# Score bias, mean times rstd and the soul shift as per-partition-scalar operations on VectorE

## Chip, cores and metric

The kernel runs on one core of one Trainium2 chip. The metric is the device time of one execution in microseconds (us), lower is better. Engines are called PE (TensorE matmul; PEld its weight loads), DVE (VectorE), ACT (ScalarE), POOL (GpSimd) and SP (the DMA-issuing SyncE).

## What is computed

128 graphs of 128 nodes with 256 features go through four layers, each with its own weights:

```
L0: softmax(q k^T / sqrt(32) + log(clip(adj, 1e-8))) v  in 8 heads, then @ Wo.T + bo, then layer_norm(x + out)
L1: p = x @ fc_w.T + fc_b ; q = p.q_w + q_b ; k = p.k_w + k_b
    masked = q + k^T + (1 - adj) * -1e9 ; leaky relu 0.01 ; softmax @ p + x
L2: scores = Q K^T / sqrt(32) + a[:, :, None] + c[:, None, :] + b_g + log(adj + 1e-9)
    with a = x @ w_g[:256], c = x @ w_g[256:] ;  softmax @ V + x
L3: as L1, with weights of its own
```

Three small steps of this matter here. The *score bias* is the sum of q_b and k_b with the node scores of L1 and L3. *Mean times rstd* is the layer norm's offset: x is normed as `x * rstd + less`, with `less = -mean * rstd`. The *soul shift* is the per-node term a (`soul` in the kernel) that is carried through the row extreme of the L2 scores.

## The kernel before

The 128 graphs are worked in 64 groups of two (`GROUP = 2`). A group passes through some 35 named steps on PE, 38 on DVE, 39 on ACT, 10 on POOL and 2 on SP. Several groups are in flight: a table `ORDER` gives, for each engine, the steps of one period with a lag, so that in the period of group t DVE does, for instance, `norm` of group t and `qk 3` of group t-3. Tables `EARLY` and `LATE` give the order at both ends. Each engine runs its list in order, and every dependence between engines is a semaphore wait written by hand ahead of the step. All matmul outputs go to eight PSUM banks of fixed use.

The steps that are touched:

- `qk` ("1" and "3" for L1 and L3), DVE, line 1092: once ACT has copied both graphs' projections to `fp` (line 839), it adds `qk_b` to the two score columns `fp[..., 256:258]`, q and k, in place, and raises `qk_ready`. PE's step `mask` (line 1313) then turns the k column of each graph into a row by two transposes, and DVE's `mask` (line 959) adds row, q column and penalty.
- `max_parts B`, DVE, lines 1006 and 1010: from the row extremes `least_B` of the L2 scores (four `max B` steps, line 1000) it makes `top = soul - least`, then `least_cols = soul - top`, with a wait of DVE on its own first instruction between the two. PE's step `turn_max B` (line 1279) transposes `least_cols_B`; ACT copies it (`least_rows_B`, line 775) and PE's `shift B` (line 1199) uses it.
- `norm`, DVE, line 1077: after POOL's power (`rstd`, line 700) one instruction makes `less` for both graphs and raises `centred`; ACT's `norm` (line 771, one instruction for each graph) writes `x_1`, and PE's `turn_x 1` (line 1285) transposes it.
- SP's loading order at the start: the first group's inputs, then eight weight tensors, then the rest.

PE also runs idle matmuls (`keep_awake`, line 1263) at both ends of the program. They write only scratch values.

Of the kernel before, what the change touches and what calls it, by code (L numbers as in the profile page):

```python
# [6 lines left out]
ALU = mybir.AluOpType  # L7
# [3 lines left out]
P = 128  # L11
GROUP = 2
# [309 lines left out]
def build_kernel(nc, ins, out):  # L322
# [4 lines left out]
    with ExitStack() as ctx:  # L327
# [36 lines left out]
        least = {"B": sb("least_B", [P, HALF, UNITS])}  # L364
        top = sb("top", [P, HALF, UNITS])
        least_cols = {s: sb(f"least_cols_{s}", [P, HALF, HEAD_DIM]) for s in "AB"}
# [77 lines left out]
        maxed = {s: sem(f"maxed_{s}") for s in "AB"}  # L444
        topped = sem("topped")
        least_ready = {"B": sem("least_ready_B")}
# [122 lines left out]
        def _(sp):  # L569
# [19 lines left out]
            load_weight("k0")  # L589
            first, *others = steps("sync")  # L590
            step(first[0], first[3])
            for n in ("o0", "f1", "k2", "q2", "f1_rows", "f3_rows", "v2", "f3"):
                load_weight(n)
            for name, _, _, G in others:
                step(name, G)
            for i in range(2):
                sp.wait_ge(stored[i], 16 * len(range(i, GROUPS, 2)))
# [112 lines left out]
        def _(act):  # L710
# [37 lines left out]
            def program():  # L748
                for name, where, n, G in steps("scalar"):
# [18 lines left out]
                    elif name == "norm":  # L768
                        act.wait_ge(centred, G.no + 1)
                        for g in range(GROUP):  # L770
# [51 lines left out]
                    elif name == "v":  # L822
                        act.wait_ge(filled[b], fills.after(G, *key))
                        if where == "0":
                            act.activation(v["A"][:, G.odd, :, :].rearrange("p g d -> p (g d)"), bank[b][:, :],
                                           ACT.Copy).then_inc(v_ready["A"], 1)
                        else:
                            act.activation(v["B"][:, G.odd, n, :], bank[b][:, 0:WIDE], ACT.Copy
                                           ).then_inc(v_ready["B"], 1)
                            if n == GROUP - 1:  # L830
                                act.wait_ge(v_ready["B"], GROUP * (G.no + 1))
                                G.wait_former(act, least_ready["B"], 1, 2)
                                act.activation(soul[:, G.odd, :], v["B"][:, G.odd, :, DIM], ACT.Identity,
                                               bias=soul_b[:, 0:1]).then_inc(soul_ready, 1)
                                act.activation(c_cols[:, :, 0:GROUP], v["B"][:, G.odd, :, DIM + 1].unsqueeze(1).broadcast_to(
                                    [P, HALF, GROUP]), ACT.Copy).then_inc(c_cols_ready, 1)
# [35 lines left out]
        def _(dve):  # L872
# [79 lines left out]
            def mask(layer, G):  # L952

                key = ("mask", layer, 0)
                b = BANK[key]
                dve.wait_ge(penalty_ready, G.no + 1)
                dve.wait_ge(filled[b], fills.after(G, *key))
# [31 lines left out]
            def program():  # L989
                for name, where, n, G in steps("vector"):  # L990
# [11 lines left out]
                    elif name == "max_parts" and where == "B":  # L1002
                        dve.wait_ge(maxed[where], HALF * (G.no + 1))
                        dve.wait_ge(soul_ready, G.no + 1)
                        a = soul[:, G.odd, :].unsqueeze(2).unsqueeze(1).broadcast_to([P, HALF, GROUP, 2])
                        dve.tensor_tensor(top[:, :, :].rearrange("p r (g h) -> p r g h", g=GROUP), a,
                                          least["B"][:, :, :].rearrange("p r (g h) -> p r g h", g=GROUP),
                                          ALU.subtract).then_inc(topped, 1)
                        dve.wait_ge(topped, G.no + 1)
                        dve.tensor_tensor(least_cols["B"][:, :, 0:UNITS].rearrange("p r (g h) -> p r g h", g=GROUP),  # L1010
                                          a, top[:, :, :].rearrange("p r (g h) -> p r g h", g=GROUP),
                                          ALU.subtract).then_inc(least_ready["B"], 1)
                    elif name == "adj_t":
# [61 lines left out]
                    elif name == "norm":  # L1075
                        dve.wait_ge(rstd_ready, G.no + 1)
                        dve.scalar_tensor_tensor(less[:, :], moments[:, :, 0], -1.0, rstd[:, :], ALU.mult, ALU.mult
                                                 ).then_inc(centred, 1)
                    elif name == "turn_x" and where != "0":
# [8 lines left out]
                    elif name == "qk":  # L1088

                        dve.wait_ge(fp_ready[where], GROUP * (G.no + 1))  # L1090
                        qk = fp[where][:, :, DIM:WIDE]
                        dve.tensor_tensor(qk, qk, qk_b[where][:, :].unsqueeze(1).broadcast_to([P, GROUP, 2]), ALU.add
                                          ).then_inc(qk_ready[where], 1)
# [13 lines left out]
        def _(pe):  # L1107
# [157 lines left out]
            def other(name, layer, n, G, to):  # L1265
# [8 lines left out]
                if name == "turn_max":  # L1274
                    if layer == "A":
                        pe.wait_ge(maxed["A"], HALF * (G.no + 1))
                    else:
                        pe.wait_ge(least_ready["B"], G.no + 1)
                    return pe.transpose(to[:, 0:P], least_cols[layer][:, :, :].rearrange("p r c -> p (r c)"),  # L1279
# [29 lines left out]
                if name == "mask":  # L1309

                    pe.wait_ge(qk_ready[layer], G.no + 1)
                    for g in range(GROUP):
# [93 lines left out]
```

## Time and profile before

| what | value |
|---|---|
| median of the runs of before | 1796.31 us (3 runs, 1795.67 to 1799.39) |
| profiled execution, first to last instruction | 1798.2 us |
| median less the profiled span | -1.9 us |
| PE busy | 1757.7 us, 98% |
| DVE busy | 1475.6 us, 82% |
| ACT busy | 1372.0 us, 76% |
| POOL busy | 731.3 us, 41% |

The profile records one execution. Busy time is a share of its span; the span is the profiled execution's own time, and no other time is recorded of it. The three runs are others, without the profiler. A row of a timeline has the start, the duration, the engine, the line and the operation with its tiles, and in brackets how long the engine sat idle before it and what ended that.

### The profile page before, as it was taken

To read this page: it belongs to the slowest core of one execution; us is meant where nothing else is said; L and a number is where in the kernel's file an instruction comes from. 1 tells how busy PE (TensorE), PEld (TensorE's weight loads), DVE (VectorE), ACT (ScalarE), POOL (GpSimd) and SP (SyncE) were. 2 spreads that over 40 slices of the span, in tenths; PEclk is the share of its full clock that TensorE was granted. 3 is DMA by queue.
4 is the path that set the end of the run, shared out by engine and by line. 5 is a ranking of instruction groups with operands and counts; after the bars stand their busy time and mean duration, and the time that the engine had idled before them with its cause. 6 is when DMAs were issued, how large, how long until landed. Compare 5 with 4: busy or idle time off the path is not lost.

```text
span 1798.2 us, 68824 instructions
## 1 busy us (share of the span) xinstructions
PE 1757.7 (98%) x28155; PEld 1647.2 (92%) x28155; DVE 1475.6 (82%) x3361; ACT 1372.0 (76%) x3792; POOL 731.3 (41%) x797
## 2 busy tenths in 40 slices
PE   7999999999999999999999999999999999999997
PEld 6899999999999999999999999999999999999986
DVE  4688888888888888888888888888888888888875
ACT  3677787777787787787787787787787787787774
POOL 3343344343443343443443343343443443443421
PEclk8999999999999999999999999999999999999999
DMA  3101011011011011011011011011011011011100
GB/s 116 39 20 49 26 49 49 26 49 50 26 49 49 26 49 49 27 49 49 26 49 50 26 49 50 26 49 49 26 49 49 26 49 49 26 49 49 35 8 25
DMA packets 48261, 74.56 MB, mean 41 GB/s; under 512 B 5456, under 2 KB 21968, under 8 KB 47952
## 3 DMA queue, kind: packets, MB, share of 16 engines
q1 hardware_dynamic: 47376, 69.49, 12.1%
q8 instruction: 228, 3.74, 0.9%
q14 instruction: 81, 0.66, 0.1%
q10 hardware_dynamic: 576, 0.68, 0.1%
HBM read 53.37 MB, written 16.78 MB: 39 GB/s over the span
## 4 chain that ended last, share of the span: by engine, by line
PE 87%; ACT 3%; DMA 3%; DVE 3%; issue 2%; POOL 2%; SPq 0%; DVEq 0%; POOLq 0%; ACTq 0%
PE banks L1111 15%; PE banks L1176 14%; PE banks L1113 13%; PE banks L1112 13%; PE banks L1325 7%; PE banks L1220 6%; PE banks L1211 6%; DMA x_t<-x_t_dram 3%; PE banks L1199 2%; PE banks L1285 2%; PE banks L1225 2%; PE banks L1313 1%; PE banks L1319 1%; POOL weights_B L684 1%; PE banks L1279 1%
## 5 line engine op out<-in xcount | busy, mean ns | idle before, releaser
L684 POOL TENSOR_TENSOR weights_B<-weights_B,adj 128x512 f32<-128x512 f32 x64 | 113.0, 1766 | 299.1 <-ACT weights_B L765 299.1
L690 POOL TENSOR_TENSOR inv_parts_A<-inv_both_A,own 128x512 fp32r<-128x512 f32 x64 | 66.7, 1042 | 303.7 <-DVE inv_both_A L1035 303.7
L1000 DVE TENSOR_REDUCE least_cols_A<-banks 128x4 f32<-128x512 f32 x256 | 159.4, 684 | 33.8 <-PE banks L1176 33.7
L1000 DVE TENSOR_REDUCE least_B<-banks 128x4 f32<-128x512 f32 x256 | 172.6, 681 | 11.6 <-PE banks L1185 11.5
L1111 PE MATMUL banks<-w_hi_v,xt_hi 128*128 128x258 f32 (+1 forms) x512 | 157.3, 307 | 9.5 <-DVE pick L883 9.5
L1111 PE MATMUL banks<-w_hi_f,xt_hi 128*128 128x258 f32 x512 | 162.3, 317 | 2.3 <-DVE xt_lo L875 0.7
L839 ACT ACTIVATE fp<-banks 128x258 f32<-128x258 f32 x256 | 92.6, 390 | 89.1 <-PE banks L1113 89.1
L765 ACT ACTIVATE banks<-banks,v_B 128x256 f32<-128x256 f32 x384 | 153.4, 474 | 0.0
L1111 PE MATMUL banks<-xt_hi,w_hi_k 128*128 128x256 f32 x512 | 150.7, 294 | 0.3 <-DVE xt_lo L875 0.3
L1113 PE MATMUL banks<-w_lo_v,xt_hi 128*128 128x258 f32 (+1 forms) x512 | 145.1, 283 | 0.0
L1112 PE MATMUL banks<-w_hi_v,xt_lo 128*128 128x258 f32 (+1 forms) x512 | 145.0, 283 | 0.0
L1113 PE MATMUL banks<-w_lo_f,xt_hi 128*128 128x258 f32 x512 | 144.9, 283 | 0.0
L1112 PE MATMUL banks<-xt_hi,w_lo_k 128*128 128x256 f32 x512 | 144.2, 282 | 0.0
L1112 PE MATMUL banks<-w_hi_f,xt_lo 128*128 128x258 f32 x512 | 143.8, 281 | 0.0
L1113 PE MATMUL banks<-xt_lo,w_hi_q 128*128 128x256 f32 x512 | 143.8, 281 | 0.0
L1111 PE MATMUL banks<-xt_hi,w_hi_q 128*128 128x256 f32 x512 | 143.7, 281 | 0.0
L1113 PE MATMUL banks<-xt_lo,w_hi_k 128*128 128x256 f32 x512 | 143.6, 280 | 0.0
L1112 PE MATMUL banks<-xt_hi,w_lo_q 128*128 128x256 f32 x512 | 143.6, 280 | 0.0
L1325 PE MATMUL banks<-fpt,fp 128*128 128x128 f32 x1024 | 142.1, 281 | 1.2 <-ACT fpt L860 1.0
L1325 PEld LDWEIGHTS banks<-fpt,fp 128*128 128x128 f32 x1024 | 128.3, 191 | 14.8 <-issue 12.4
L1024 DVE TENSOR_TENSOR weights_A<-banks,adj 128x512 f32<-128x512 f32 x192 | 125.7, 683 | 9.2 <-ACT banks L761 9.2
L1031 DVE RECIPROCAL banks<-banks 128x128 f32<-128x128 f32 x128 | 122.4, 956 | 9.3 <-PE banks L1220 9.3
(192 smaller groups left out, 6172.0 us busy)
## 6 DMA issues: line engine op xcount, KB each, us to landing
x_t<-x_t_dram SPq DMA_DIRECT2D x64, 256.0 KB, 3.6
x_in<-x_dram SPq DMA_DIRECT2D x64, 256.0 KB, 3.6
out_dram<-x_out SPq DMA_DIRECT2D x64, 256.0 KB, 2.4
adj_t<-adj_t_dram SPq DMA_DIRECT2D x64, 128.0 KB, 3.4
adj<-adj_dram SPq DMA_DIRECT2D x64, 128.0 KB, 2.0
scratch<-weights_dram SPq DMA_DIRECT2D x9, 256.0 KB, 6.6
scratch<-weights_dram ACTq DMA_DIRECT2D x2, 256.0 KB, 4.3
out_bias<-L_gnn_bo_dram ACTq DMA_DIRECT2D x1, 128.0 KB, 7.8
```

Source lines behind the costliest of these rows:

```text
L684: pool.tensor_tensor(units, units, weight_of[where][:, G.four, :, :].unsqueeze(2).broadcast_to([P, GROUP, 2, P]), ALU.mult).then_inc(first ...
L765: last = act.activation(to[:, cols(g, 2 * P)], x[:, cols(g, 2 * P)], ACT.Exp, bias=v["B"][:, G.odd, g, DIM + 1:WIDE], scale=-1.0)
L1000: dve.tensor_reduce(to, bank[SCORE_BANKS[n]].rearrange("p (u m) -> p u m", u=UNITS), axis=AX.X, op=ALU.min).then_inc(maxed[where], 1)
L1024: dve.tensor_tensor(weights[where][:, n, :].rearrange(units, g=GROUP, h=2), bank[SCORE_BANKS[n]].rearrange(units, g=GROUP, h=2), weight_of ...
L1031: dve.reciprocal(bank[b][:, 0:P], bank[b][:, 0:P]).then_inc(inverted[where], 1)
L1111: pe.matmul(out_ap, left_hi(k), right_hi(k), start=(k == 0), stop=False)
L1112: pe.matmul(out_ap, left_lo(k), right_hi(k), start=False, stop=False)
L1113: last = pe.matmul(out_ap, left_hi(k), right_lo(k), start=False, stop=(k == KT - 1))
L1176: last = pe.matmul(bank[SCORE_BANKS[r]][:, cols(u)], left[row_group(r), G.odd, half, cols(g)], right[row_group(r), G.odd, half, cols(g)], ...
L1211: last = pe.matmul(to[row_group(r), cols(u)], v[s][:, G.odd, g, head:head + HEAD_DIM], weights[s][:, r, cols(u)], start=True, stop=True)
L1220: last = pe.matmul(to[row_group(r), 0:P], sums[:, u, :], weights[s][:, r, cols(u)], start=(u == 0), stop=(u == UNITS - 1), skip_group_chec ...
L1325: last = pe.matmul(to[:, cols(k * GROUP + g)], fp[layer][:, g, cols(k)], fpt[layer][:, g, :], start=True, stop=True)
```

## The change

`qk` becomes one `tensor_scalar` for each layer that adds both biases (two per-partition scalars) to the q column alone; PE's `mask` step no longer waits for it, but only for ACT's `fp`, and DVE's `mask` step waits for it by name. `max_parts B` becomes two `tensor_scalar`, one for each graph, that subtract and add `soul` and don't depend on each other; tile `top` and its semaphore are gone. `norm` becomes two `tensor_scalar`, one for each graph. All steps keep their places. SP's start is written as another loop with the same order.

```diff
-        top = sb("top", [P, HALF, UNITS])
...
-                        act.wait_ge(centred, G.no + 1)
+                        act.wait_ge(centred, GROUP * (G.no + 1))
...
-                                G.wait_former(act, least_ready["B"], 1, 2)
+                                G.wait_former(act, least_ready["B"], GROUP, 2)
...
                 b = BANK[key]
+                dve.wait_ge(qk_ready[layer], G.no + 1)
                 dve.wait_ge(penalty_ready, G.no + 1)
...
-                        a = soul[:, G.odd, :].unsqueeze(2).unsqueeze(1).broadcast_to([P, HALF, GROUP, 2])
-                        dve.tensor_tensor(top[:, :, :].rearrange("p r (g h) -> p r g h", g=GROUP), a,
-                                          least["B"][:, :, :].rearrange("p r (g h) -> p r g h", g=GROUP),
-                                          ALU.subtract).then_inc(topped, 1)
-                        dve.wait_ge(topped, G.no + 1)
-                        dve.tensor_tensor(least_cols["B"][:, :, 0:UNITS].rearrange("p r (g h) -> p r g h", g=GROUP),
-                                          a, top[:, :, :].rearrange("p r (g h) -> p r g h", g=GROUP),
-                                          ALU.subtract).then_inc(least_ready["B"], 1)
+                        for g in range(GROUP):
+                            dve.tensor_scalar(least_cols["B"][:, :, 2 * g:2 * g + 2], least["B"][:, :, 2 * g:2 * g + 2],
+                                              soul[:, G.odd, g:g + 1], soul[:, G.odd, g:g + 1],
+                                              ALU.subtract, ALU.add).then_inc(least_ready["B"], 1)
...
-                        dve.scalar_tensor_tensor(less[:, :], moments[:, :, 0], -1.0, rstd[:, :], ALU.mult, ALU.mult
-                                                 ).then_inc(centred, 1)
+                        for g in range(GROUP):
+                            dve.tensor_scalar(less[:, g:g + 1], moments[:, g, 0:1], rstd[:, g:g + 1], -1.0,
+                                              ALU.mult, ALU.mult).then_inc(centred, 1)
...
-                        qk = fp[where][:, :, DIM:WIDE]
-                        dve.tensor_tensor(qk, qk, qk_b[where][:, :].unsqueeze(1).broadcast_to([P, GROUP, 2]), ALU.add
+                        q = fp[where][:, :, DIM]
+                        dve.tensor_scalar(q, q, qk_b[where][:, 0:1], qk_b[where][:, 1:2], ALU.add, ALU.add
                                           ).then_inc(qk_ready[where], 1)
...
-                        pe.wait_ge(least_ready["B"], G.no + 1)
+                        pe.wait_ge(least_ready["B"], GROUP * (G.no + 1))
...
-                    pe.wait_ge(qk_ready[layer], G.no + 1)
+                    pe.wait_ge(fp_ready[layer], GROUP * (G.no + 1))
```

DVE in a middle period, from the last `max B` to the L3 `mask`, before the change (in brackets the semaphores that the instruction waits for):

```order
L1000 TENSOR_REDUCE least_B<-banks 128x4 [waits filled0]
L1092 TENSOR_TENSOR fp<-fp,cols_tile 128x2x2 [waits fp_ready_3]
L1006 TENSOR_TENSOR top<-soul,least_B 128x16 [waits soul_ready,maxed_B]
L1010 TENSOR_TENSOR least_cols_B<-soul,top 128x4x4 [waits topped]
L1041 TENSOR_TENSOR banks<-banks,heads_A 128x512 [waits filled5,heads_ready_A]
L986 TENSOR_TENSOR sum_t<-banks,xb_t 128x512 [waits filled6,x3_ready,x_biased_1]
L959 SCALAR_TENSOR_TENSOR logits<-banks,fp,penalty 128x128 [waits filled7,penalty_ready]
```

The same stretch of DVE after the change:

```order
L998 TENSOR_REDUCE least_B<-banks 128x4 [waits filled0]
L1087 TENSOR_SCALAR fp<-fp,cols_tile 128x2 [waits fp_ready_3]
L1004 TENSOR_SCALAR least_cols_B<-least_B,soul 128x4x2 [waits soul_ready,maxed_B]
L1004 TENSOR_SCALAR least_cols_B<-least_B,soul 128x4x2
L1035 TENSOR_TENSOR banks<-banks,heads_A 128x512 [waits filled5,heads_ready_A]
L984 TENSOR_TENSOR sum_t<-banks,xb_t 128x512 [waits filled6,x3_ready,x_biased_1]
L957 SCALAR_TENSOR_TENSOR logits<-banks,fp,penalty 128x128 [waits filled7,penalty_ready,qk_ready_3]
```

The count of instructions is the same here; the wait for `topped` is gone, and the first `mask` instruction has `qk_ready_3` as a third wait.

DVE around `norm` in the same period, before the change:

```order
L1072 TENSOR_SCALAR rstd<-moments 128x1 [waits stats_ready,moments_ready,x1_ready]
L1074 BN_AGGR moments<-stats 128x2
L1087 RECIPROCAL f_inv<-f_den 128x2 [waits f_exped_3]
L1077 SCALAR_TENSOR_TENSOR less<-moments,rstd 128x2 [waits rstd_ready]
L1000 TENSOR_REDUCE least_cols_A<-banks 128x4 [waits filled0] x4
```

And after it:

```order
L1066 TENSOR_SCALAR rstd<-moments 128x1 [waits stats_ready,moments_ready,x1_ready]
L1068 BN_AGGR moments<-stats 128x2
L1082 RECIPROCAL f_inv<-f_den 128x2 [waits f_exped_3]
L1072 TENSOR_SCALAR less<-moments,rstd 128x1 [waits rstd_ready]
L1072 TENSOR_SCALAR less<-moments,rstd 128x1
L998 TENSOR_REDUCE least_cols_A<-banks 128x4 [waits filled0] x4
```

There is one instruction more ahead of the four `max A`.

PE around the L3 `mask` and `turn_max B`, before the change:

```order
L1325 MATMUL banks<-fpt,fp 128x128 x3
L1313 MATMUL banks<-ident,fp 128x128 [waits qk_ready_3,fpt_ready_1]
L1313 MATMUL banks<-ident,fp 128x128
L1279 MATMUL banks<-ident,least_cols_B 128x128 [waits least_ready_B,fp_ready_3]
L1176 MATMUL banks<-qt_B,kt_B 128x128 [waits maxed_B]
```

And after it:

```order
L1320 MATMUL banks<-fpt,fp 128x128 x3
L1308 MATMUL banks<-ident,fp 128x128 [waits fp_ready_3,fpt_ready_1]
L1308 MATMUL banks<-ident,fp 128x128
L1274 MATMUL banks<-ident,least_cols_B 128x128 [waits least_ready_B,fp_ready_3]
L1171 MATMUL banks<-qt_B,kt_B 128x128 [waits maxed_B]
```

Nothing moves on PE; one wait names ACT's semaphore instead of DVE's.

## Rows read from the trace of the kernel before

**Rows 1.** The page: busy time, share of the span and instructions of each engine.

```profile
PE 1757.7 (98%) x28155; PEld 1647.2 (92%) x28155; DVE 1475.6 (82%) x3361; ACT 1372.0 (76%) x3792; POOL 731.3 (41%) x797
```

**Rows 2.** Windows: stretch, length, busy by engine, PE clock share, DMA share, GB/s.

```profile
0.00:60.00 60.00, 44.21 (x484) 40.33 (x485) 29.26 (x70) 24.50 (x55) 21.21 (x47) 0.86 0.31 102
800.00:1200.00 400.00, 398.93 (x6502) 375.46 (x6495) 340.10 (x774) 316.74 (x880) 170.05 (x178) 1.00 0.13 40
1200.00:1600.00 400.00, 396.45 (x6489) 372.81 (x6491) 335.88 (x769) 313.04 (x869) 167.65 (x177) 1.00 0.13 42
1740.00:1798.20 58.20, 47.39 (x627) 41.44 (x625) 33.40 (x73) 31.30 (x91) 10.83 (x12) 1.00 0.05 20
```

**Rows 3.** PE's waits, whole span: waited for, us in total, times, longest.

```profile
PE banks L1285 <- ACT x L771: 9.0, 12, 1.6
...
PE banks L1279 <- DVE least_cols_B L1010: 0.2, 1, 0.2
PE banks L1313 <- DVE fp L1092: 0.2, 1, 0.2
```

**Rows 4.** PE's waits in the window 400 to 1600 us, all of them.

```profile
PE banks L1285 <- ACT x L771: 5.9, 8, 1.6
PE banks L1225 <- POOL inv_parts_B L690: 0.2, 1, 0.2
```

**Rows 5.** Timeline around `qk 3` and `max_parts B` of a middle period.

```profile
923.60 0.16 DVE L1092 TENSOR_TENSOR fp<-fp,cols_tile 128x4 f32<-128x4 f32 x1 [0.30 <-ACT fp L839]
923.67 0.17 DVE L1006 TENSOR_TENSOR top<-soul,least_B 128x16 f32<-128x16 f32 x1
923.88 0.17 DVE L1010 TENSOR_TENSOR least_cols_B<-soul,top 128x16 f32<-128x16 f32 x1
923.98 0.69 DVE L1041 TENSOR_TENSOR banks<-banks,heads_A 128x512 f32<-128x512 f32 x1
...
924.10 0.38 PE L1313 MATMUL banks<-ident,fp 128*128 128x128 f32 x2
...
924.31 0.27 PE L1279 MATMUL banks<-ident,least_cols_B 128*128 128x128 f32 x1
```

**Rows 6.** Timeline around `norm` in a period where PE waited.

```profile
717.77 0.16 DVE L1077 SCALAR_TENSOR_TENSOR less<-moments,rstd 128x2 f32<-128x2 f32 x1 [1.10 <-POOL rstd L700]
...
718.45 2.48 DVE L1000 TENSOR_REDUCE least_cols_A<-banks 128x4 f32<-128x512 f32 x4 [0.52 <-PE banks L1176]
...
720.16 0.63 ACT L794 ACTIVATE xt_hi<-x_t 128x512 fp32r<-128x512 f32 x1 [1.15 <-DMA x_t<-x_t_dram]
...
720.70 1.07 ACT L771 ACTIVATE x<-x,less,rstd 128x256 f32<-128x256 f32 x2
...
721.91 0.63 PE L1285 MATMUL banks<-ident,x 128*128 128x128 f32 x4 [0.73 <-ACT x L771]
```

**Rows 7.** Chain that ended last, at the last group's `qk 3`: start, us, what.

```profile
1787.66 0.40 ACT fp L839
1788.06 0.02 issue
1788.08 0.18 DVE fp L1092
1788.26 0.04 issue
1788.30 0.45 PE banks L1313 x2
```

**Rows 8.** The same chain at the first group's `max_parts B`.

```profile
85.47 0.47 DVE top L1006
...
85.96 0.18 DVE least_cols_B L1010
```

**Rows 9.** Waits: who waited for `less`, in total, times, longest.

```profile
ACT x L771 <- DVE less L1077: 1.9, 3, 1.0
```

**Rows 10.** DVE groups by form: busy us, mean ns, then idle time before.

```profile
L1035 DVE SCALAR_TENSOR_TENSOR inv_both_B<-banks,low_row,inv_hi_B 128x128 f32<-128x128 f32 x64 | 22.5, 351 | 2.2
...
L1072 DVE TENSOR_SCALAR rstd<-moments 128x1 f32<-128x1 f32 x64 | 9.8, 154 | 5.8
```

More of the change, by code:

```diff
@@ L444, in build_kernel @@
         maxed = {s: sem(f"maxed_{s}") for s in "AB"}
-        topped = sem("topped")
         least_ready = {"B": sem("least_ready_B")}
@@ L589, in _ @@
             load_weight("k0")
[L590 to L594, printed above, removed]
+            for i, (name, _, _, G) in enumerate(steps("sync")):
                 step(name, G)
+                if i == 0:
+                    for n in ("o0", "f1", "k2", "q2", "f1_rows", "f3_rows", "v2", "f3"):
+                        load_weight(n)
             for i in range(2):
```

## The prediction

> **What bounds the kernel now.** I read the page's first part first: PE is busy for 1757.7 of 1798.2 us, DVE for 82% [rows 1]. A high busy share alone can mislead, since it is a mean over stages, so the second view is the table of windows. In the middle of the program PE is busy for 398.9 and 396.5 us of two stretches of 400 us; at the two ends it is busy for 44.2 of 60.0 and 47.4 of 58.2 us [rows 2]. The reader is to see two different regimes: a middle in which a DVE edit can win only what PE waits there, and two ends in which single instructions lie one behind another.
>
> The third view is the list of what PE waited for. In the 1200 us from 400 to 1600 it has two entries: ACT's `x` (step `norm`), 5.9 us in 8 waits, and a POOL tile, 0.2 us in one wait [rows 4]. None names DVE. Over the whole span the two DVE products that the change touches and PE reads, `least_cols_B` and `fp`, held PE up once each, for 0.2 us [rows 3]. So 128 `mask` steps and 64 `turn_max B` steps on PE have practically no wait to give back.
>
> The one large wait does touch an edited step: `turn_x 1` on PE for ACT's `x`, 9.0 us in 12 waits [rows 3]. The timeline of such a period tells why it happens. `less` was written at 717.93 (717.77 plus 0.16), but ACT began `x` only at 720.70, because ACT first stood 1.15 us for the DMA of `x_t`, which its preceding instruction needs [rows 6]. The transfer is late, not `less`. ACT waited for `less` only 3 times in 64 groups, 1.9 us in all [rows 9].
>
> **The change, part by part.**
>
> *Score bias.* One DVE instruction stands for one, of 0.16 us before [rows 5]; the new one handles 2 elements instead of 4, and the nearest tensor_scalar, on one element, takes 154 ns [rows 10]. DVE's time is unchanged. What changes is that PE's `mask` starts after ACT's `fp`. In the middle `qk 3` ends at 923.76 and PE takes up the transposes at 924.10 [rows 5], behind its own matmuls: 0.34 us of cover, nothing gained. In the last group the pair is on the chain: ACT's `fp` ends at 1788.06, DVE's bias takes 1788.08 to 1788.26, PE begins at 1788.30 [rows 7]. Without the bias in between PE begins at about 1788.10, if its hand-over from ACT takes the 0.04 us that it takes from DVE: a gain of 0.20 us, once. The bias is then done beside the transposes (0.45 us [rows 7]), and DVE's `mask`, which now waits for it by name, finds it done. Behind this wait on DVE stand `mask`, `weigh` and `leak`; as DVE works in order, the bias, issued ahead of them, has been finished for long in the middle too.
>
> *Soul shift.* Two instructions stand for two. Before, the second began 0.21 us after the first (923.67 to 923.88), while the next instruction, which doesn't depend on it, followed after 0.10 (923.88 to 923.98), and the first had itself followed `qk` after 0.07 (923.60 to 923.67) [rows 5]. The self-wait thus costs some 0.11 us. After: the second ends at about 923.67 + 0.09 + 0.16 = 923.92 instead of 924.05, 0.13 us sooner. PE wants the tile at 924.31 [rows 5], so nothing is gained in the middle, and DVE's own 0.1 us in each group goes into its idle share. In the first group the pair is on the chain, 0.47 and 0.18 us [rows 8]; I take 0.15 us of gain there. The bounds are none, if the 0.47 us is a cost of the first execution of that place in the program, and 0.4, if it goes away with the chain.
>
> The Trainium skill ("VectorE: DVE Perf Modes", section "The DRAIN you can't avoid") holds that a semaphore after each of a row of DVE instructions costs nothing over one at the end. By it the 0.15 us would be zero and the sum 0.15 us higher. This trace doesn't agree for these tiny dependent instructions: 0.21 against 0.10 us from start to start [rows 5].
>
> *Mean times rstd.* One instruction becomes two. Its price in DVE's stream is one more start-to-start distance, 0.07 to 0.10 us as above [rows 5]; I take 0.09, and 0.18 as an upper end, when the second shows the whole instruction. In the middle DVE sits idle for 0.52 us right behind `less`, until PE's scores are there [rows 6], so the four `max A` begin at the same time as before. ACT has room as well: without its 1.15 us for the DMA it would have begun `x` at 719.55 instead of 720.70, still 1.6 us after `less` was there [rows 6]. On the path it lies in the places where ACT did wait, three of them [rows 9]: 3 times 0.09 is 0.27 us of loss, at most 0.54.
>
> *SP's loop, the tile and the semaphore that go* change no order. I put them at nothing.
>
> **The sum.** -0.20 (bias, last group) -0.15 (soul shift, first group) +0.27 (mean times rstd, three places) is -0.08 us against a profiled execution of 1798.2 us. Its span lies 1.9 us above the median of the three runs, which is more than the whole effect, so I carry the difference to the median: 1796.31 - 0.08 is **1796.2 us**. The bounds of the terms, taken all to one side, are -0.20 - 0.4 + 0 = -0.6 and 0 + 0 + 0.54 = +0.5 us.
>
> **Rivals.**
>
> *Slower, because a new pair ends after PE wants it.* This has one place, `turn_max B`. No row shows a DVE instruction with two per-partition scalars. The nearest with one is `inv_both`, 351 ns, though on 128 elements [rows 10]; the longest in this place is 0.47 us [rows 8]. The point that decides is 924.31, where PE takes up the tile: the pair now ends 0.26 us ahead of it [rows 5]. With 0.47 us and a second start to start of 0.47 the second ends at 924.61, 0.30 us too late, in each of 64 groups: 19 us, 1815 us. Against it: 128 elements alone account for much of the 351 ns, and eight elements are little; the one-element tensor_scalar takes 154 ns [rows 10]. 0.03.
>
> *Slower, by the number of instructions.* 64 more DVE instructions at 0.09 us are 5.8 us, 1802.1 us, if DVE's stream set the pace. It decides where less than 0.09 us of idle time follows `less`; the row shows 0.52 [rows 6], and PE's list has no DVE entry [rows 4]. 0.02. The Trainium skill (same page, section "Rules for kernel authors") advises to minimise the count of operations rather than of semaphores, which speaks for this rival; the rows of this kernel say that DVE has room for them.
>
> *Faster, by the whole wait for `x`.* If the 12 waits were owed to `less`, or if DVE's 0.1 us per group brought the `x_t` transfer forward, up to 9.0 us [rows 3] would come back: 1787.3 us. Against it: the releaser is the DMA [rows 6], and that is issued by SP in an order and behind waits that the change leaves alone. 0.03.
>
> *Nothing at all at the ends.* The chain has other branches within tenths of a microsecond, so that the -0.20 and -0.15 may be swallowed and the +0.27 too: 1796.3 us. This can't be told apart from my forecast by a timing; it shares its chance.
>
> **How the numbers follow.** The three runs of before lie 3.7 us apart, 0.2%; a change below about 0.2%, 3.6 us, can't be told from no change. My forecast, with the case of nothing at the ends, has 0.92, and falls within 0.2% unless the runs themselves stray. The rivals have 0.03, 0.02 and 0.03. I move 0.01 more to each side for edges at which DVE's slightly shifted stream meets a bank or a transfer in a way that the rows don't show: faster 0.04, same 0.90, slower 0.06. The range holds the forecast, the -0.6 and +0.5 of the terms and a spread like that of the runs: 1796.31 - 0.6 - 1.5 is 1794.2, and 1799.39, the slowest run of before, less a little, 1798.9. The rivals with 0.08 lie outside.
>
> **What the next profile would show.** Right: PE's waits between 400 and 1600 us again with no DVE entry and some 6 us for `x`; DVE's instructions up by 64; starts of the soul pair 0.07 to 0.10 us apart; `less` twice and still idle time behind it; on the last chain ACT's `fp` handing over to PE directly. Wrong: a wait of PE for `least_cols_B` in many groups with per-partition-scalar instructions of 0.3 us or more (first rival); the idle time ahead of `max A` gone (second); the `x` waits gone (third).

## The result, and the profile after

The changed kernel takes 1815.26 us (median of 4 runs, 1813.92 to 1815.87) against 1797.37 us for the kernel before on the same chip (4 runs, 1795.67 to 1799.39): a ratio of 1.0098, 95% interval 1.0084 to 1.0112. It is 1% slower. The forecast was 1796.2 us, no change.

The page of the changed kernel, its head and first part (busy time, share of the span, instructions):

```profile
span 1813.3 us, 68888 instructions
...
PE 1772.2 (98%) x28155; PEld 1652.8 (91%) x28155; DVE 1509.9 (83%) x3425; ACT 1372.6 (76%) x3792; POOL 730.6 (40%) x797
```

The profiled execution took 15.1 us more than the one before [rows 1]. PE's share is still 98%, since its busy time has grown by 14.5 us as well. PE did no more work: there are 28155 matmuls in both, and between 400 and 1600 us their mean length is 0.28 us in both. But these records overlap. A matmul is drawn that long while the next usually starts 0.12 us behind it, so PE can be held for a tenth or two without a gap between two records. The share says nothing of the loss. The list of what PE waited for from 400 to 1600 us (engine, tile and line, what ended the wait; us in total, times, longest) says hardly more:

```profile
PE banks L1280 <- ACT x L768: 4.6, 6, 1.2
PE banks L1106 <- DVE xt_lo L872: 0.4, 1, 0.4
PE banks L1274 <- DVE least_cols_B L1004: 0.2, 1, 0.2
```

Beside [rows 4] the DVE tile of the soul shift has appeared, but with one wait of 0.2 us, and 15 us are missing. The same list for the weight loads of the changed kernel has a trace of it, under a name that accuses nobody:

```profile
PEld banks L1171 <- issue: 17.2, 81, 0.3
...
PEld banks L1274 <- issue: 3.9, 23, 0.4
```

The kernel before has no row for `turn_max B` (L1279) in this list. Its row for the scores is longer, not shorter, so that row is no part of the loss:

```profile
PEld banks L1176 <- issue: 20.9, 123, 0.3
```

The view that does show it is the timeline around DVE's `qk 3` and `max_parts B`, the place of [rows 5], in the changed kernel:

```profile
955.07 0.29 DVE L1087 TENSOR_SCALAR fp<-fp,cols_tile 128x2 f32<-128x2 f32 x1 [0.32 <-ACT fp L836]
955.27 0.48 DVE L1004 TENSOR_SCALAR least_cols_B<-least_B,soul 128x8 f32<-128x8 f32 x2
955.46 0.25 PEld L1308 LDWEIGHTS banks<-ident,fp 128*128 128x128 f32 x2
...
955.65 0.69 DVE L1035 TENSOR_TENSOR banks<-banks,heads_A 128x512 f32<-128x512 f32 x1
955.86 0.14 PEld L1274 LDWEIGHTS banks<-ident,least_cols_B 128*128 128x128 f32 x1
```

and the two weight loads of the same place in the kernel before, which [rows 5] leave out:

```profile
923.99 0.25 PEld L1313 LDWEIGHTS banks<-ident,fp 128*128 128x128 f32 x2
...
924.21 0.14 PEld L1279 LDWEIGHTS banks<-ident,least_cols_B 128*128 128x128 f32 x1
```

From the start of the bias to the end of the soul pair it is 0.68 us now (955.07 to 955.75); before it was 0.45 (923.60 to 924.05 [rows 5]). The weight load of `turn_max B` follows the pair after 0.11 us now and followed after 0.16 before. So DVE is 0.23 us longer, the first 0.05 us of that were free here, and the rest is PE's: from the first weight load of `mask` to that of `turn_max B` it is 0.40 us where it was 0.22.

The groups of instructions with their shapes, of the changed kernel (count | busy us, mean ns of one | idle before):

```profile
L1087 DVE TENSOR_SCALAR fp<-fp,cols_tile 128x2 f32<-128x2 f32 x128 | 36.4, 284 | 20.8 <-ACT fp L836 20.8
L1004 DVE TENSOR_SCALAR least_cols_B<-least_B,soul 128x8 f32<-128x8 f32 x128 | 31.1, 288 | 0.3
L1029 DVE SCALAR_TENSOR_TENSOR inv_both_B<-banks,low_row,inv_hi_B 128x128 f32<-128x128 f32 x64 | 22.5, 351 | 2.2
L1072 DVE TENSOR_SCALAR less<-moments,rstd 128x1 f32<-128x1 f32 x128 | 21.4, 209 | 64.4 <-POOL rstd L697 64.4
L1066 DVE TENSOR_SCALAR rstd<-moments 128x1 f32<-128x1 f32 x64 | 9.8, 154 | 6.2 <-DVE moments L1061 0.4
```

The bias instruction, priced by a neighbour of 154 ns, takes 284. The second place that it hurts is `qk 1`, which DVE does ahead of the first row of `weigh A` and `mask 1`. In the changed kernel:

```profile
945.83 0.28 DVE L1087 TENSOR_SCALAR fp<-fp,cols_tile 128x2 f32<-128x2 f32 x1
946.02 1.28 DVE L1018 TENSOR_TENSOR weights_A<-banks,adj 128x512 f32<-128x512 f32 x2
...
947.74 0.68 DVE L1018 TENSOR_TENSOR weights_A<-banks,adj 128x512 f32<-128x512 f32 x1
...
948.01 0.25 PEld L1314 LDWEIGHTS banks<-ident,logits 128*128 128x128 f32 x2
...
948.53 0.90 PEld L1171 LDWEIGHTS banks<-kt_B,qt_B 32*128 32x128 f32 x28 [0.27 <-issue]
```

And in the kernel before:

```profile
914.49 0.15 DVE L1092 TENSOR_TENSOR fp<-fp,cols_tile 128x4 f32<-128x4 f32 x1
914.55 1.28 DVE L1024 TENSOR_TENSOR weights_A<-banks,adj 128x512 f32<-128x512 f32 x2
...
916.27 0.68 DVE L1024 TENSOR_TENSOR weights_A<-banks,adj 128x512 f32<-128x512 f32 x1
...
916.69 0.24 PEld L1319 LDWEIGHTS banks<-ident,logits 128*128 128x128 f32 x2
...
917.10 0.98 PEld L1176 LDWEIGHTS banks<-kt_B,qt_B 32*128 32x128 f32 x32 [0.17 <-issue]
```

The scores of half B overwrite the bank that the last `weigh A` reads. They begin 0.11 us after its end now (948.42 to 948.53) and began 0.15 after it (916.95 to 917.10). The bracket reads "issue" in both kernels, 0.27 us for 0.17. The prediction never looked at this place.

Because the waits hide under weight loads, the rest of this text measures PE by distances: from the first weight load of a step to the first of the next, mean over the 43 whole periods between 400 and 1600 us of each profile, in us. `turn_p` to scores B is the second place (the step is `turn_p 3`, which stands ahead of scores B in PE's order; the expectations below call it `turn_p 1`), `mask 3` to `turn_max B` the first, "col to den" is from the column terms of scores B to `den A`, "x" from the projection ahead of `turn_x 1` to it, where PE waits for ACT's `x`. e1 to e11 are the experiments below.

```
        period  turn_p to  col to   mask 3 to    turn_max B   x
                scores B   den      turn_max B   to again B
before  26.993  0.420      0.457    0.228        0.306        0.907
after   27.242  0.496      0.481    0.408        0.259        0.864
e1      27.105  0.503      0.480    0.301        0.260        0.857
e2      26.988  0.420      0.455    0.301        0.260        0.863
e3      26.903  0.417      0.456    0.232        0.306        0.801
e4      27.040  0.435      0.482    0.340        0.259        0.797
e5      26.941  0.412      0.457    0.222        0.307        0.854
e6      27.133  0.413      0.450    0.220        0.310        0.834
e7      27.111  0.502      0.480    0.220        0.309        0.847
e8      26.934  0.419      0.449    0.221        0.308        0.849
e9      27.087  0.514      0.482    0.225        0.307        0.873
e10     27.067  0.418      0.454    0.296        0.259        0.894
e11     27.009  0.449      0.481    0.221        0.309        0.814
```

The column x scatters by 0.1 us from profile to profile whatever the kernel. The changed kernel's period is 0.249 us longer: +0.180 and -0.047 around `turn_max B`, +0.076 and +0.024 around scores B, -0.043 in x, and +0.059 in many steps of 0.02 us and less. Because x scatters, kernels are better compared by the period less x: +0.292 us for the changed kernel, which times 62 periods is 18 us, about the measured difference. Over the whole program, the 55 periods from the start of the fifth group's scores A (121.7 us in the profile before) to that of the sixtieth (1607.4) are 12.5 us longer, what lies behind them 3.2 longer, the start 0.6 shorter; together 15.1. The 3.2 us are mostly middle periods too: at the last scores B (1766.6 us before) the changed kernel is 14.1 us late, so only about 1 us falls behind that.

### The profile page after: what moved, and what is told of

Same layout as the page of the kernel before. It is cut to its first block, busy times and chain, and to the rows that moved or that the text cites. A ratio compares the mean times of both kernels' runs of the same rounds, so it can differ in the third digit from the quotient of the medians.

```text
span 1813.3 us, 68888 instructions
## 1 busy us (share of the span) xinstructions
PE 1772.2 (98%) x28155; PEld 1652.8 (91%) x28155; DVE 1509.9 (83%) x3425; ACT 1372.6 (76%) x3792; POOL 730.6 (40%) x797
## 4 chain that ended last, share of the span: by engine, by line
PE 87%; DVE 4%; DMA 2%; ACT 2%; issue 2%; POOL 2%; SPq 0%; DVEq 0%; POOLq 0%; ACTq 0%
PE banks L1106 16%; PE banks L1171 14%; PE banks L1108 13%; PE banks L1107 13%; PE banks L1320 7%; PE banks L1215 6%; PE banks L1206 6%; PE banks L1194 2%; DMA x_t<-x_t_dram 2%; PE banks L1220 2%; PE banks L1280 2%; PE banks L1314 2%; PE banks L1308 1%; PE banks L1274 1%; PE banks L1180 1%
```

## The experiments

The theory after the result: an instruction with per-partition scalars costs DVE more than the plain form, and at two places PE waits for DVE's stream with next to no slack. Its rivals: the cost is the changed waits (PE's `mask` for `fp`, DVE's `mask` by name); or it is the number of instructions; or the longer x path. Each ratio is to the kernel before as timed beside it on the same chip, with the 95% interval.

**e1, the bias part alone**, in the kernel before:

```diff
+                dve.wait_ge(qk_ready[layer], G.no + 1)
...
-                        qk = fp[where][:, :, DIM:WIDE]
-                        dve.tensor_tensor(qk, qk, qk_b[where][:, :].unsqueeze(1).broadcast_to([P, GROUP, 2]), ALU.add
+                        q = fp[where][:, :, DIM]
+                        dve.tensor_scalar(q, q, qk_b[where][:, 0:1], qk_b[where][:, 1:2], ALU.add, ALU.add
...
-                    pe.wait_ge(qk_ready[layer], G.no + 1)
+                    pe.wait_ge(fp_ready[layer], GROUP * (G.no + 1))
```

> The kernel before with the score bias alone as changed (bias instruction with two per-partition scalars, PE's mask step waiting for fp only). Theory H (hand-over): PE takes up scores B and turn_max B no sooner than 0.11 to 0.12 us after the DVE instruction that it waits for; before, both stood at 0.15, so 0.04 us was all the slack. The new bias instruction holds DVE 0.19 instead of 0.07 us from start to start, once ahead of the weigh A that scores B waits for and once ahead of the soul pair: 0.08 us each per group, some 0.05 of the second given back behind turn_max B. 0.11 us x 62 groups is 7 us: 1804 us, ratio 1.0035 to 1.005. Rival N (the extra norm instruction is the cause): no change, 1797. Rival P (PE's own changed wait is the cause, whatever DVE's instruction costs): the whole 17 us here, 1815.

1806.61 us, ratio 1.0057 (1.0040 to 1.0074), just above the range that was expected. **e2, the soul part alone** (the hunks of the change for `max_parts B`, `top` left in place):

> The kernel before with the soul shift alone as changed. Theory H: the pair ends 0.10 us later than before (0.55 instead of 0.45 us after the start of the bias instruction ahead of it), of which 0.04 is slack and about 0.05 is given back behind turn_max B: 0 to 1.5 us in all, 1797 to 1799. Rival S (the soul pair alone is the cause, as the first rival of the prediction had it): 12 to 19 us, 1810 to 1816. Rival N: no change.

1799.66 us, 1.0017 (1.0006 to 1.0029). **e3, the norm part alone**:

> The kernel before with mean times rstd alone as changed. Theory H: hidden by the idle time behind it, 0.30 us of which is left in the changed kernel: within 1 us of before, 1797. Rival N (64 more DVE instructions set the pace): 6 to 17 us, 1803 to 1814.

1794.51 us, 0.9995 (0.9984 to 1.0005). The parts add up to 0.69% where the whole costs 0.98%. The table says where the rest is. At `turn_max B` each of e1 and e2 is +0.073 and is given back 0.045 right behind it, a net of 0.03; both together are +0.180 and give back the same 0.047, a net of 0.13. What is given back comes once, whatever the size, so the two parts cost 0.08 us more together than apart, 62 times 0.08 is 5 us or 0.28%. (The intervals of the three parts leave the sum of 0.69% open by about 0.2%; the distances are sharper.)

**e4, one scalar instead of two**: in the changed kernel the sum of the two biases is formed once, in the setup.

```diff
+                    dve.tensor_tensor(q_b[n][:, :], qk_b[n][:, 0:1], qk_b[n][:, 1:2], ALU.add).then_inc(setup_dve, 1)
...
-                        dve.tensor_scalar(q, q, qk_b[where][:, 0:1], qk_b[where][:, 1:2], ALU.add, ALU.add
+                        dve.tensor_scalar(q, q, q_b[where][:, 0:1], None, ALU.add
```

> The changed kernel with one edit: the two biases are summed once at the start, so the bias instruction has one per-partition scalar instead of two. Theory H with a price by the number of per-partition scalars: DVE's duration of the bias falls from 284 to about 206 ns and its start to start from 0.19 to 0.12 us; 0.07 us less at each of two places per group, 4 to 9 us of the 17 come back: 1806 to 1811. If the price lay in the instruction's kind and not in its scalars: 1815, duration 284.

**e5, no scalar**: the kernel before with the new waits of e1 and that summed column, as a tensor_tensor.

```diff
+                        q = fp[where][:, :, DIM]
+                        dve.tensor_tensor(q, q, q_b[where][:, :].broadcast_to([P, GROUP]), ALU.add
```

> The kernel before with PE's mask step waiting for fp only and the bias on the q column alone, as in the change, but as a tensor_tensor with a column that holds the sum of both biases (summed once at the start), so without a per-partition scalar. Theory H (the price lies in the per-partition scalars, and PE meets it at two hand-overs): DVE's bias takes 156 ns again, PE's distance from turn_p 1 to scores B is 0.42 us again (0.50 with the changed bias), and the time is that of before within 0.15%: 1793 to 1798. Rival P (what costs is that PE waits for ACT's fp instead of DVE): 1806, as with the bias change alone.

e4 is 1806.83 us, 1.0057 (1.0041 to 1.0073); e5 is 1798.08 us, 1.0008 (0.9999 to 1.0017). The groups of the bias in e4, and then in e5:

```profile
L1090 DVE TENSOR_SCALAR fp<-fp,q_b 128x2 f32<-128x2 f32 x128 | 28.7, 224 | 21.0 <-ACT fp L837 21.0
```

```profile
L1096 DVE TENSOR_TENSOR fp<-fp,q_b 128x2 f32<-128x2 f32 x128 | 20.2, 158 | 19.6 <-ACT fp L840 19.6
```

On the same two elements: 158, 224 and 284 ns with no, one and two per-partition scalars. From its start to that of DVE's next instruction it is 0.07, 0.13 and 0.19 us. One scalar less in the changed kernel gives back 0.41% (1.0098 to 1.0057); 0.06 us at 128 places is 7.7 us, 0.43%. With e5 the new waits are acquitted: its distances are those of the kernel before. So is the other rival, as far as it is one of counts: in its periods e4 has as many instructions as the changed kernel.

**e6, the last `weigh A` ahead of `mask 1`** in DVE's order of the kernel before. This asks whether scores B is held by DVE for more than the change added.

```diff
-        (3, "sum", "2", 0), (1, "qk", "1", 0), (0, "weigh", "A", 1), (0, "weigh", "A", 2), (1, "mask", "1", 0),
-        (0, "weigh", "A", 3), (1, "leak", "1", 0), ...
+        (3, "sum", "2", 0), (1, "qk", "1", 0), (0, "weigh", "A", 1), (0, "weigh", "A", 2), (0, "weigh", "A", 3),
+        (1, "mask", "1", 0), (1, "leak", "1", 0), ...
```

> The kernel before with one exchange in DVE's order: the third weigh A of a group ahead of mask 1 in the middle periods. Theory H says that PE's scores B is held by this weigh in the kernel before too: its distance from turn_p 1 falls from 0.42 to 0.22 to 0.30 us, 0.12 to 0.2 us per group, 7 to 12 us in all: 1784 to 1789, if what DVE does next has room for mask 1 being 0.6 us later (0.2 us of idle time ahead of max B and 0.3 us ahead of the L3 bias speak for that). Rival: scores B was not held by DVE (the trace names no releaser there): no change at scores B, 1795. Third possibility: scores B starts sooner but the delay of leak 1 reappears at wide A or turn_max B, and the time stays or grows.

1806.97 us, 1.0054 (1.0041 to 1.0066). The gain of 7 to 12 us that was expected is not there: with `weigh A` done a whole instruction sooner, scores B still begins 0.413 us after `turn_p` (0.420 before). In the kernel before DVE holds PE by hundredths at this place at most. The loss is elsewhere: DVE's `mask 1` comes later, DVE then stands 0.52 us ahead of `leak 1`, in the period shown, until ACT has answered it. What follows in DVE's order is late, POOL's `inv_parts_A` with it, and `wide A` on PE begins 0.213 us later in each period (mean distance ahead of it 0.916 for 0.703). The rows of DVE and POOL, of e6:

```profile
945.51 0.42 DVE L968 TENSOR_TENSOR logits<-banks,logits 128x256 f32<-128x256 f32 x1 [0.52 <-ACT banks L842]
...
949.92 1.04 POOL L690 TENSOR_TENSOR inv_parts_A<-inv_both_A,own 128x512 fp32r<-128x512 f32 x1 [4.95 <-DVE inv_both_A L1035]
951.09 0.19 PEld L1225 LDWEIGHTS banks<-inv_parts_A,spread 128*128 128x128 f32 x1
```

**e7, `max_parts B` ahead of `qk 3`** in DVE's order of the changed kernel:

```diff
-        (3, "qk", "3", 0), (2, "max_parts", "B", 0), ...
+        (2, "max_parts", "B", 0), (3, "qk", "3", 0), ...
```

> The changed kernel with one exchange in DVE's order: the L3 bias behind the soul pair instead of ahead of it (PE's mask no longer waits for the bias). Theory H: the pair ends 0.19 us sooner, PE's distance from the L3 mask to turn_max B falls from 0.41 to about 0.23 us, of which 0.05 was given back behind it: 0.13 us per group, 8 us less than the changed kernel, 1805 to 1808, ratio to before 1.0045 to 1.007. If this hand-over were not on PE's path: 1815.

1805.65 us, 1.0046 (1.0034 to 1.0059). `mask 3` to `turn_max B` falls from 0.408 to 0.220, the level of before, with the two-scalar pair as slow as ever: some 0.5% of the 0.98% came from this place.

**e8, the bias on POOL**: the kernel before with the waits of e5 and the bias of both layers in POOL's order.

```diff
+                        pool.tensor_tensor(q, q, q_b[where][:, :].broadcast_to([P, GROUP]), ALU.add
+                                           ).then_inc(qk_ready[where], 1)
```

> As the tensor_tensor bias, but done by POOL (in gaps of its order where it waits for DVE or ACT), so that DVE has no bias at all. Theory H: DVE reaches the weigh A that scores B waits for 0.07 us sooner than before, and the soul pair too: turn_p 1 to scores B 0.42 to 0.35 us, the L3 mask to turn_max B 0.23 to 0.21: 0.07 to 0.09 us per group, 4 to 6 us less than before: 1790 to 1792. Rival: POOL delivers the bias too late for DVE's mask and the time grows by some microseconds.

1795.43 us, 0.9990 (0.9981 to 0.9999). The expected gain of 4 to 6 us did not come. With no bias on DVE at all the two distances are what they were, and the gain is 0.1%: from the level of before the way down is flat.

**e9 and e10, two spare instructions without scalars** ahead of DVE's `qk 1` (e9) and of `qk 3` (e10) in the kernel before. They write a tile that nobody reads:

```diff
+                            for i in range(2):
+                                dve.tensor_tensor(spare[:, i, :], one[:, :].broadcast_to([P, 2]),
+                                                  big[:, :].broadcast_to([P, 2]), ALU.add)
```

> The kernel before with two more DVE instructions (tensor_tensor on 2 elements of tiles that nothing else uses, no per-partition scalar) ahead of the L1 bias of every group. They hold DVE for 2 x 0.07 = 0.14 us, a little more than the 0.12 us by which the changed bias is longer. Theory H: scores B goes 0.10 us later (turn_p 1 to scores B 0.42 to 0.52), 6 us in all, 1803, ratio 1.003 to 1.004. Rival: DVE's room absorbs it, since the kernel before has 4 us of DVE idle time per group: 1796.

> As the run before it, but the two instructions stand ahead of the L3 bias. Theory H: turn_max B goes 0.10 us later (L3 mask to turn_max B 0.23 to 0.33), of which 0.05 is given back behind it: 3 us, 1798 to 1800, ratio 1.001 to 1.003. Rival: absorbed, 1796.

e9 is 1805.77 us, 1.0051 (1.0039 to 1.0063); e10 is 1803.11 us, 1.0041 (1.0029 to 1.0053). Plain instructions that hold DVE for 0.14 to 0.15 us lengthen the same distances by about as much as the scalars' 0.12 us: +0.094 and +0.025 around scores B (e1 +0.083 and +0.023), +0.068 ahead of `turn_max B` (e1 +0.073). It is DVE's lateness that counts, whatever it is made of. In time both came out above the ranges expected, and together they cost 0.92% where e1 costs 0.57%. For e10 a part of that can be read from its trace: in the kernel before, PE's `mask 3` still waits for DVE's bias. In e10 it begins 0.116 us after the bias ends in the mean, 0.115 at least (0.224 or more before), which is the least distance that a hand-over takes here, and the step ahead of it is 0.029 us longer. So e10 holds a third hand-over, which the changed kernel doesn't have.

**e11, e4 and e7 together**:

> The changed kernel with both remedies: the biases summed once, so that the bias instruction has one per-partition scalar, and the L3 bias behind the soul pair. Theory H: scores B 0.43 us after turn_p 1 and turn_max B 0.22 us after the L3 mask, as before; the time is that of before within 0.2%: 1795 to 1800. If something else in the change cost time (the norm instruction, the sum of small shifts elsewhere), some microseconds stay.

1801.48 us, 1.0023 (1.0013 to 1.0034), a little more than expected. `turn_max B` is at the level of before; scores B, which was expected at 0.43 us, keeps +0.029 and +0.024, since the one scalar is still there. The rest is 0.01 us here and there, in projections, `mix` and the output projection.

**e12, `x_t` earlier**: from the third group on, SP issues a group's `x_t` ahead of its `adj` in the kernel before, not behind it. This tests how the prediction read PE's one large wait.

```diff
-                    G.wait_former(sp, xt_ready["0"], 1, 1)
-                    sp.dma_start(x_t[:, :], ins["x_t"][G.no]).then_inc(xt_landed, 16)
+                    if G.no < 2:
+                        G.wait_former(sp, xt_ready["0"], 1, 1)
+                        sp.dma_start(x_t[:, :], ins["x_t"][G.no]).then_inc(xt_landed, 16)
...
+                    if 0 < G.no < GROUPS - 1:
+                        sp.wait_ge(xt_ready["0"], G.no + 1)
+                        sp.dma_start(x_t[:, :], ins["x_t"][G.no + 1]).then_inc(xt_landed, 16)
```

> The kernel before with one transfer moved in SP's order: from the third group on x_t of the next group is issued ahead of the adj transfer that waits for POOL's penalty step, so some 20 us sooner. It tests the prediction's reading that PE's waits for ACT's x (9.0 us in 12 waits) are owed to late x_t transfers. If so, these waits nearly vanish from the trace, PE's distance from den B to turn_x falls from 0.91 us to 0.8 or below in the mean, and the time falls by 4 to 8 us: 1789 to 1793, ratio 0.9955 to 0.998. If they are owed to something else (ACT's own queue): 1796.

1792.42 us, 0.9975 (0.9966 to 0.9984), faster than both kernels. PE's wait for `x` and, from the groups by line, ACT's for the transfer, of e12:

```profile
PE banks L1289 <- ACT x L775: 1.7, 3, 1.0
```

```profile
L798 ACT ACTIVATE xt_hi<-x_t 128x512 fp32r<-128x512 f32 x64 | 40.3, 630 | 0.8 <-DMA x_t<-x_t_dram 0.8
```

The same group of ACT in the kernel before:

```profile
L794 ACT ACTIVATE xt_hi<-x_t 128x512 fp32r<-128x512 f32 x64 | 40.4, 631 | 12.9 <-DMA x_t<-x_t_dram 12.9
```

9.0 us in 12 waits [rows 3] have become 1.7 in 3, and ACT's wait for the transfer has gone from 12.9 to 0.8 us. The distance x is 0.72 us in the mean (0.91 before), the other distances are those of before. DVE's part in `norm` is untouched.

## Why the prediction was wrong

**The step that failed is the price of the bias**: "the new one handles 2 elements instead of 4, and the nearest tensor_scalar, on one element, takes 154 ns [rows 10]. DVE's time is unchanged." That neighbour has immediates for operands. The bias takes 284 ns and holds up the next instruction by 0.19 us for 0.07. The trace of the kernel before had the price, in two pairs of instructions of the setup that differ only in this: line 913 takes a per-partition scalar (`minus_gamma`) for one layer and an immediate for the other.

```profile
L913 DVE SCALAR_TENSOR_TENSOR w_lo_f<-banks,minus_gamma,w_hi_f 128x2 fp32r<-128x2 f32 x2 | 0.3, 214 | 1.9 <-ACT w_hi_f L732 1.9
L913 DVE SCALAR_TENSOR_TENSOR w_lo_f<-banks,w_hi_f 128x2 fp32r<-128x2 f32 x2 | 0.2, 149 | 0.0
```

That is 65 ns for one scalar on two elements. Two of them on the 159 ns of the old bias give an estimate of 289; 284 and 288 were measured. `inv_both`, with one per-partition scalar, 351 ns on 128 elements [rows 10], says the same. DVE's big forms here give the cost of an element: 683 ns on 512 and 422 on 256 is 1.02 ns each; 128 of them are 131 ns, which leaves 220 for the scalar form. e4 measured 224. The prediction waved it off with "128 elements alone account for much of the 351 ns" and didn't do this subtraction. The soul shift fell with it: each of its pair takes 288 ns, so from its own start the pair takes 0.48 us for the 0.38 of the old form, and ends 0.10 later, not 0.13 sooner. The self-wait that it saves is less than the scalars cost (e2).

**The cover was read at the wrong row.** The "0.26 us ahead" and "0.34 us of cover" run up to the start of the matmuls (924.31, 924.10 [rows 5]). What waits first is the weight load, 924.21, and a load never followed its DVE instruction by less than 0.11 us. The slack was 924.21 less 0.11 less 924.05, 0.05 us here; over 45 periods the mean distance was 0.147 us where the floor is 0.115 (0.114 to 0.116 in all 44 periods of the changed kernel), so 0.03. About the same slack stood at scores B (0.150 for 0.115), which the prediction didn't visit at all. "None names DVE" was true of the list of waits and told little, since a hold of a tenth of a microsecond is put down to "issue" or covered by overlapping records.

**The first rival was right in its kind.** It named the place (`turn_max B`), the form (two per-partition scalars), and the sign that would show it, "instructions of 0.3 us or more" (0.28 and 0.29), and gave 1815 us for the 1815.26 measured, at a chance of 0.03. The closeness of the number is luck: its 19 us were 0.30 us at one place; what happened is 0.13 net there, 0.10 at scores B and 0.06 in small steps, in each period. Its price should have been 65 ns for each scalar, and its point of decision 0.05 us, not 0.26; both could be read from the trace of the kernel before, and with them a loss was to be forecast. Its second sign, "a wait of PE for `least_cols_B` in many groups", did not appear between 400 and 1600 us (one wait named, 23 as "issue").

**The second rival**, by the number of instructions, is not what happened: e3 adds the same 64 instructions and costs nothing. The place decides: 128 instructions more ahead of `qk 1` (e9) cost 0.51%. The Trainium skill ("VectorE: DVE Perf Modes", section "Rules for kernel authors") advises to minimise the count of operations. Taken alone that would have pointed at `norm`, the one part with more instructions, and these runs don't bear it out there; e4 has the count of the changed kernel in its periods and is 0.4% faster.

**Mean times rstd** was right: room behind `less`, no change (0.9995). In the changed kernel, ACT's waits for `less`, then the timeline behind it:

```profile
ACT x L768 <- DVE less L1072: 2.2, 3, 1.2
```

```profile
937.73 0.33 DVE L1072 TENSOR_SCALAR less<-moments,rstd 128x1 f32<-128x1 f32 x2 [1.10 <-POOL rstd L697]
938.37 2.48 DVE L998 TENSOR_REDUCE least_cols_A<-banks 128x4 f32<-128x512 f32 x4 [0.30 <-PE banks L1171]
```

Three waits again, 2.2 us for 1.9 [rows 9], +0.3 as the +0.27 of the sum (three waits are few, and e3's time can't tell a term of this size from none), and 0.30 us of idle time left for 0.52 [rows 6]. The instruction is 209 ns where one on the same single element with immediates alone is 154, one scalar's worth more. The third rival was rightly refused: e12 shows that the `x` waits belong to the transfer.

**The bias on the last chain** was right in kind. In the chain that ended last, the L3 transposes now stand behind PE's own idle matmuls (L1258, `keep_awake`) with nothing of DVE between, unlike [rows 7]:

```profile
1802.91 0.48 PE banks L1258 x4
1803.39 0.44 PE banks L1308 x2
1803.83 0.03 issue
```

PE's own rows have the gain. From the start of the idle matmuls behind the last projection to the first transpose it was 0.84 us before and is 0.63 now, 0.21 us sooner where 0.20 was forecast; the changed kernel's rows:

```profile
1802.75 0.64 PE L1258 MATMUL banks<-w_hi_q 128*128 128x256 f32 x4
1803.38 0.43 PE L1308 MATMUL banks<-ident,fp 128*128 128x128 f32 x2
```

and the same place in the kernel before:

```profile
1787.46 0.64 PE L1263 MATMUL banks<-w_hi_q 128*128 128x256 f32 x4
1788.30 0.43 PE L1313 MATMUL banks<-ident,fp 128*128 128x128 f32 x2 [0.20 <-DVE fp L1092]
```

Beside 18 us it can't be seen in the time. The soul shift's -0.15 in the first group went the other way. The chain there in the changed kernel:

```profile
84.78 0.04 DVE least_cols_B L1004
84.82 0.34 issue
85.15 0.29 DVE least_cols_B L1004
85.45 0.14 issue
85.58 0.30 PE banks L1274
```

From 84.78 to 85.45 it is 0.67 us for the 0.47 and 0.18 of [rows 8]: no gain. The second of the pair starts 0.37 us after the first, against 0.19 in the middle, though it waits for nothing of the first. That speaks for the prediction's bound "a cost of the first execution of that place"; no run tests it.

**Shown and open.** Shown: the scalars' price (e4, e5), the two places (e7 for the first, e9 for the second, e10), and that at scores B the kernel before lies at a kink, flat below and steep above (e5, e6, e8 on the one side, e1, e9 on the other). The 0.047 us that are given back ahead of the second scores of B can be read from the traces. Their first weight load starts 0.071 to 0.073 us before the drawn end of the `turn_max B` matmul, in every middle period of all fourteen profiles. Where `turn_max B` was not held, its matmul starts 0.104 us behind its own weight load and is drawn 0.274 long (mean of the kernel before); where it was held, 0.031 behind and 0.300 long (changed kernel). That puts its end 0.047 us nearer to its weight load, however long the hold was.

Open: why some steps (projections, the step ahead of `mask 3`) are 0.01 to 0.02 us longer in the changed kernel, e4, e7 and e11, and not in the parts alone. All four of these kernels also lack tile `top` and have SP's other loop, which the prediction put at nothing and e1 to e3 leave out. No run separates these, so up to some 0.06 us of each period, 3 to 4 us of the 18, may be theirs.

## What to carry to other kernels

Price a small DVE instruction by its operands, not by its elements: look for a row with the same kind of operands, in the setup too, and take the elements off a larger one (ns per element from two sizes) when there is none of that size. Before saying that PE has cover, measure from the end of the producing instruction to PE's weight load, not to its matmul, subtract the smallest such distance in the trace, and do it at every PE step behind the edited one on its engine, weights and freed banks too. An engine list without an entry for DVE is no evidence of slack: a tuned kernel can sit where hundredths are free and the next tenth is paid in every period.

## What the runs showed of the hardware

- A per-partition scalar costs a small VectorE instruction about 60 ns: 158, 224 and 284 ns for none, one and two on 128x2 (e5, e4, after), and 0.07, 0.13, 0.19 us to the next start. For a scalar_tensor_tensor on 128x2 it is 149 ns with an immediate and 214 with one scalar (before); for a tensor_scalar on 128x1, 154 ns with immediates only and 209 with one scalar (after).
- From the end of the VectorE instruction to the weight load that waits for it, at `turn_max B` and scores B, there are never less than 0.114 us in the middle of any of these traces; where PE does wait, it is 0.114 to 0.116 us in every period (after).
- The weight load of the scores starts 0.071 to 0.073 us before the drawn end of the `turn_max B` matmul ahead of it (all traces).
- Such waits are mostly invisible as waits: between 400 and 1600 us, with periods 0.249 us longer, one wait of PE for an edited DVE product was named, 0.2 us; 3.9 us stood as "issue" of a weight load, and PE's busy time over the program grew by 14.5 us with the same 28155 matmuls.
